# Decoder layer, quantised feed-forward stage: a maximum taken from the SBUF copy, a row of the final norm placed later, four banks for the last tiles

## The reference, cut to what matters

```python
def act_quant(x):
    scale = 127.0 / jnp.clip(jnp.max(jnp.abs(x), axis=-1, keepdims=True), EPS)
    return jnp.clip(jnp.round(x * scale), -128.0, 127.0) / scale

def h_bitlinear(x, w):                    # fwht: Hadamard transform of the last axis
    return jnp.einsum('bsh,oh->bso', act_quant(fwht(x)), weight_quant(w))

gate = h_bitlinear(hidden_states, w_gate)         # 512 -> 2048
up = h_bitlinear(hidden_states, w_up)
out = h_bitlinear(jax.nn.silu(gate) * up, w_down) # 2048 -> 512
...
x = _layernorm(x + _L0_attn_ref(...), axis=-1)
x = _layernorm(x + _L0_xattn_ref(...), axis=-1)
x = _layernorm(x + _L0_ffn_ref(...), axis=-1)
```

## Time and profile before

| | |
|---|---|
| median of 3 runs | 1088.88 us (1086.02 to 1090.52) |
| the profiled execution | 1086.8 us, of which 1084.9 from the first to the last instruction (the span) |
| TensorE busy | 936.8 us (86%) |
| VectorE busy | 875.3 us (81%) |
| ScalarE busy | 678.9 us (62.6%) |
| GpSimd busy | 231.3 us (21%) |
| mean granted TensorE clock | 0.959 of full speed |

### The profile page before, as it was taken

One profiled execution on the slowest core, in us unless ns is written; L12 is line 12 of the kernel. 1 busy time (PEld: TensorE's weight loads), 2 busy tenths in 40 slices (PEclk: granted clock), 3 DMA queues, 4 the chain that ended last, 5 costly groups with the idle time before them and its releaser, 6 DMA issues. The chain is left out here.

```text
span 1084.9 us, 13454 instructions
## 1 busy us (share of the span) xinstructions
PE 936.8 (86%) x4128; PEld 358.6 (33%) x4128; DVE 875.3 (81%) x1670; ACT 678.9 (63%) x1115; POOL 231.3 (21%) x248
## 2 busy tenths in 40 slices
PE   3567699999999999999898879897989889889966
PEld 1223233322222222222222444353444334343422
DVE  7997688899999999999897589658755776578467
ACT  3787688888888889877666234354524553275351
POOL 4203411122222331232201422140005000320001
PEclk9688899999999999999999999999999999999988
DMA  8956765566666556664442323120233004100501
GB/s 328 383 179 238 222 177 162 178 190 197 190 196 192 162 175 196 197 184 144 132 123 91 116 70 75 41 104 1 60 96 117 1 7 139 48 2 3 172 20 39
DMA packets 90684, 145.00 MB, mean 134 GB/s; under 512 B 12339, under 2 KB 52147, under 8 KB 89078
## 3 DMA queue, kind: packets, MB, share of 16 engines
q1 hardware_dynamic: 90614, 144.16, 42.3%
HBM read 84.75 MB, written 42.21 MB: 117 GB/s over the span
## 5 line engine op out<-in xcount | busy, mean ns | idle before, releaser
L402 DVE TENSOR_REDUCE neg_max<-banks 128x1 f32<-128x512 f32 x512 | 327.7, 682 | 32.8 <-PE banks L374 29.2
L1396 ACT ACTIVATE probs<-banks 128x512 f32<-128x512 f32 x512 | 277.1, 606 | 76.7 <-PE banks L1299 75.8
L1313 PE MATMUL banks<-probs,v_st 128*32 128x512 f32 x1024 | 137.9, 612 | 0.6 <-ACT probs L1396 0.6
L1850 PE MATMUL banks<-q_T,f_int_all 128*128 128x512 bf16 x512 | 122.9, 379 | 14.1 <-DVE h_ring L1871 10.1
L374 PE MATMUL banks<-attn_T,x_T 96*128 96x512 bf16 x256 | 98.6, 393 | 19.6 <-DVE neg_max L402 13.6
L1195 POOL TENSOR_TENSOR rstd<-vare,half 128x1 f32<-128x1 f32 x48 | 29.2, 608 | 401.1 <-DVE vare L1187 401.1
L1865 ACT ACTIVATE h_ring<-h_ring 128x512 f32<-128x512 f32 x64 | 40.3, 630 | 106.1 <-DVE h_ring L1860 106.1
L374 PE MATMUL banks<-k_st,q_st 96*128 96x512 bf16 x256 | 98.3, 384 | 7.8 <-DVE neg_max L402 6.4
L1299 PE MATMUL banks<-q_st,k_st 99*128 99x512 bf16 x256 | 96.0, 383 | 3.8 <-ACT probs L1396 1.8
L1299 PE MATMUL banks<-x_T,attn_T 99*128 99x512 bf16 x256 | 97.9, 382 | 0.1
L409 POOL TENSOR_TENSOR rest<-y,parts 128x512 f32<-128x512 f32 x32 | 37.6, 1174 | 211.7 <-ACT parts L382 211.6
(11 more groups left out here) (286 smaller groups left out, 1555.1 us busy)
## 6 DMA issues: line engine op xcount, KB each, us to landing
f_int_all<-in_ffn_dram SPq DMA_DIRECT2D x24, 512.0 KB, 7.6
qk_parts<-parts SPq DMA_DIRECT2D x32, 384.0 KB, 2.6
woT<-in_ffn_dram SPq DMA_DIRECT2D x24, 512.0 KB, 6.5
qk_parts<-parts SPq DMA_DIRECT2D x32, 256.0 KB, 2.9
pv_rows<-pv_z SPq DMA_DIRECT2D x32, 256.0 KB, 5.5
hz<-h_turned SPq DMA_DIRECT2D x32, 256.0 KB
x_T<-qk_parts SPq DMA_DIRECT2D x16, 384.0 KB, 3.9
attn_T<-qk_parts SPq DMA_DIRECT2D x16, 384.0 KB, 4.9
```

What stands on the lines that cost most here:

```text
L402: dve.tensor_reduce(neg_max[:, g.h, tile:tile + 1], s_bank[(16 * g.n + tile) % SB], AX.X, ALU.max, negate=True).then_inc(max_done, 1)
L1313: last = pe.matmul(pv_bank[32 * j:32 * j + 32, :], v_st[g.v][:, kt].rearrange("p h d -> p (h d)")[:, (HD + 1) * head:(HD + 1) * head + 2 * ...
L1396: act.activation(probs[ktp][:, j, i, :], st_bank[(16 * g.n + 2 * w + i) % STB], ACT.Exp).then_inc(exp_done, 2)
L1850: last = pe.matmul(bank, f_int[w][:, k * FF + ch.start:k * FF + ch.stop], q1_T[:, k, :], start=k == 0, stop=k == KD - 1)
```

## The change

Three things. **The maximum**: ScalarE no longer writes magnitudes; it only copies each pair into `hz`. VectorE reads the copy: one TENSOR_REDUCE takes the larger magnitude of the pair's two blocks, 1024 elements in, 512 out, through a view in which the two elements of each result lie 512 elements apart, and for every pair but the first a TENSOR_TENSOR of 128x512 puts it into `h_max`. The waits that named the magnitudes name the copy. **The row**: for b = 1 and 2 the final row 3 of batch b - 1 moves from step 15 of the first stage, where it stood ahead of the x2 read of row 0, to behind row 0's norm in the second stage; its scaling moves behind the x2 read of row 1, and its step on GpSimd moves with it. The x2 read now waits for the final row that used its own part of the buffer. **The last tiles**: in the last batch the four down tiles get four banks, and ScalarE rounds tiles 2 and 3, VectorE tiles 0 and 1.

```diff
@@ dve_xm
-            if n == 0:
-
-                need(dve, "d_read", 4 * (B - 1))
+            if B >= 2:
+                need(dve, "d_read", 4 * (B - 2) + n + 1)
@@ constants and banks
-            ACT_TILE, DVE_TILES = 2, (0, 1, 3)
+            ACT_TILES, DVE_TILES = (2, 3), (0, 1)
...
             def down_bank(b, t):
-                return psum[6 + t % 2] if b >= NB - 2 else LOW
+                return psum[t] if b == NB - 1 else psum[6 + t % 2] if b == NB - 2 else LOW
@@ pe_gate_up
                         if i < 2:
-                            need(pe, "h_abs", 8 * b)
+                            need(pe, "h2_sb", 8 * b)
@@ act_y
-                if i == KD:
-                    need(act, "maxed", 16 * b)
@@ pe_h2
                 else:
-                    need(pe, "h_abs", 8 * b + p - 1)
+                    need(pe, "h2_sb", 8 * b + p - 1)
@@ act_h2, dve_max
-            def magnitudes(p):
-                return h_abs[:] if p % 2 == 0 else y_own[:, 0:2, :]
-
             def act_h2(act, b, p):
                 need(act, "h2_mm", 8 * b + p + 1)
                 did(act.copy(hz[:, 2 * p:2 * p + 2, :], pair_banks(p)), "h2_sb")
-                need(act, "maxed", 16 * b + 2 * p - 2)
-                need(act, "bias_o_ready", 2)
-                did(act.activation(magnitudes(p), pair_banks(p), ACT.Abs), "h_abs")
 
             def dve_max(dve, b, p):
-                need(dve, "h_abs", 8 * b + p + 1)
-                for a in range(2):
-                    n = 16 * b + 2 * p + a
-                    need(dve, "maxed", n)
-                    if p == 0 and a == 0:
-                        need(dve, "top_mm", b)
-                        did(dve.tensor_copy(h_max[:], magnitudes(p)[:, a, :]), "maxed")
-                    else:
-                        did(dve.tensor_tensor(h_max[:], magnitudes(p)[:, a, :], h_max[:], ALU.max), "maxed")
+                need(dve, "h2_sb", 8 * b + p + 1)
+                if p == 0:
+                    need(dve, "top_mm", b)
+                out = h_abs[:, p % 2, :] if p else h_max[:]
+                did(dve.tensor_reduce(out, hz[:, 2 * p:2 * p + 2, :].rearrange("p a s -> p s a"), AX.X, ALU.max,
+                                      apply_absolute_value=True), "h_part")
+                if p:
+                    need(dve, "h_part", 8 * b + p + 1)
+                    need(dve, "maxed", 7 * b + p - 1)
+                    did(dve.tensor_tensor(h_max[:], out, h_max[:], ALU.max), "maxed")
@@ pe_top
-                need(pe, "maxed", 16 * b + 16)
-                need(pe, "h_abs", 8 * b + 7)
+                need(pe, "maxed", 7 * b + 7)
+                need(pe, "h2_sb", 8 * b + 7)
@@ act_half_q2
-                need(act, "q2_round", 2 * (NB - 1) + part + 1)
+                need(act, "q2_round", 2 * (NB - 1) + 2 * ACT_TILES.index(t) + part + 1)
@@ pe_down
-                    if b >= NB - 2:
+                    if b == NB - 1:
+                        need(pe, "h2_sb", 8 * NB)
+                    elif b == NB - 2:
@@ dve_first
-                    if b and down_end(b, i - 1) is not None:
+                    if b and i < FK - 1 and down_end(b, i - 1) is not None:
                         dve_final(dve, b - 1, down_end(b, i - 1))
...
                 dve_h(dve, b, FK - 1)
-                if b and b < NB - 1:
-                    dve_final_norm(dve, b - 1, KD - 1)
@@ dve_second
                 dve_xm_norm(dve, B, 0)
+                if b:
+                    dve_final(dve, b - 1, KD - 1)
                 dve_xm(dve, B, 1, FRONT)
+                if b:
+                    dve_final_norm(dve, b - 1, KD - 1)
@@ pool_second
                 pool_rstd(pool, 1, 4 * B)
+                if b:
+                    pool_final(pool, b - 1, KD - 1)
@@ the scalar block, last batch
-                    for part in range(2):
-                        act_half_round(act, ACT_TILE, part)
-                        act_half_q2(act, ACT_TILE, part)
+                    for t in ACT_TILES:
+                        for part in range(2):
+                            act_half_round(act, t, part)
+                            act_half_q2(act, t, part)
@@ the vector block, last batch
-                            if t != ACT_TILE:
+                            if t in DVE_TILES:
                                 dve_half_q2(dve, t, part)
```

More of the change, by code:

```diff
@@ L2003, in half_made @@
                 at = 2 * (NB - 1) + part + 1
-                return ("q2_ready", at) if t == ACT_TILE else ("q2_dve", at + 2 * DVE_TILES.index(t))
+                return ("q2_ready", at + 2 * ACT_TILES.index(t)) if t in ACT_TILES else ("q2_dve", at + 2 * DVE_TILES.index(t))
             def dve_half_scale(dve, t, part):
```

## The result

The changed kernel takes 1071.92 us (median of 4 runs, 1068.55 to 1077.68) against 1089.38 of the kernel before (4 runs, 1086.02 to 1090.52): a ratio of 0.986, 95% interval 0.983 to 0.988. The forecast was 1099 us, 0.9% slower. The profiled execution has a span of 1066.6 us against 1084.9.

A forecast was written before the change was run, and what follows sets the result against it. No engine is full; the chain goes to and fro between TensorE, ScalarE and VectorE. The terms 14.7 + 5.4 - 6.6 - 3.4 = 10.1 us slower gave 1099 us, range 1073 to 1111.

The forecast's parts named there:

- R: Duration of VectorE's new reduce, 1024 elements in, 512 out: taken as 1.98 us; break-even at 1.67.
- rival (a): VectorE's new reduce reads apart at the full rate, R = 1.21: 14.6 us won, 1074.3 us; chance 0.25.
- The three rows with inputs apart: Traced reduces with inputs 32 or 8 elements apart: 224 elements 0.529 us, 128 elements 0.369, 32 elements 0.207.
- The other sign: GpSimd's work next to VectorE's reduces lengthens them, by up to 0.4 us for each of three pairs.
- The second stages: Three second stages at R = 1.98: dve_quant2 starts at 34.25 us, not 29.34; 4.9 us lost each, 14.7 in all.
- the prediction's own walk: VectorE's second-stage list timed in order, gaps of 0.04 us; at R = 1.21, dve_quant2 comes 1.3 us earlier.
- Its slope: Between the ends, each second stage moves by eight times the change of R.
- A pair's pitch: VectorE's time per pair in a second stage: 1.98 + 0.69 + gaps, 2.74 us.
- The last pairs: Last batch's reduces and maxima on VectorE end at 1056.3, not 1050.93: 5.4 us lost, or 0.7 earlier at R = 1.21.
- The row: x2 read 1.80 us earlier; TensorE waits 1.2, not 3.02, eight matmuls 3.60, not 5.11: 6.6 us won in two stages.
- The last tiles: Last batch's tail: TensorE no longer waits for the final row; tile 3 ends at 1075.6, not 1079.0: 3.4 us won.
- rival (b): R from 1.5 to 1.84, two alternating places served better: within 5.4 us, taken as 1089; chance 0.12.

The follow-up runs named there:

- e4_probe: Changed kernel with twenty magnitude reduces added at its very end (one run); 224 elements in groups of seven took 0.54 us apart, 0.40 adjacent.
- e6_longer: Changed kernel with one more VectorE reduce per pair, 512 elements to 1, result not used: 1083.0 us, ratio 0.995 to the kernel before.
- e2: Kernel before with only final row 3 moved behind the x2 read: 1078.8 us, ratio 0.991.
- e1: Kernel before with only the maximum changed (ScalarE copies, VectorE reduces the copy): 1074.1 us against 1088.0, ratio 0.987.
- e11: Kernel before with only the maximum changed, plus unused matmuls put into TensorE's waits: 1069.3 us, ratio 0.981.
- e8: Changed kernel with unused matmuls put into TensorE's waits: 1062.9 us, ratio 0.977 to the kernel before.
- e7_probe2: Changed kernel with nineteen more VectorE instructions at its very end (one run); reduces in groups of 3 took 1.34 us, of 5 1.89.

## Why the prediction was wrong, step by step

**R.** The step that failed is "I take 1.98 us, from L215: a group of four is nearest to two". It is 1.23 us, and 1.21, the value of rival (a), was the one to take. The three rows with inputs apart were read rightly as slower for being apart (the line through them, 1.87 us for 1024, is what groups of four, eight and sixteen take in e4_probe to 0.03), but the rule was carried over to a group length that it doesn't hold for. The three rows differ from the new reduce in group length, and the prediction took the nearest length as near enough; groups of two, apart by 128 bytes, 2 KB or 16 KB, take what adjacent ones take. The other sign that the prediction named, reduces made longer by GpSimd's work beside them, did not come: all 32 took 1.22 to 1.24 us.

**The second stages.** Forecast 14.7 us lost; measured 0.6, 1.15 and 0.8, 2.6 us won. With R = 1.21 the prediction's own walk gave 1.3 each, 3.9. Without the lower clock a stage won 1.8, so the walk was too low there, and what the measured stages lack of it is the clock: the walk had TensorE slow only at the transposes, while in the changed kernel the slow stretch lay on the gate and up group ahead of them and held them up. Its slope, eight times the change of R, was too steep: e6_longer shows half against the changed kernel, and 0.7 of it against stages at full clock. Two terms of the walk were mis-sized. A pair's pitch at R = 1.23 is 1.87 and not about 2.0, since the gap ahead of an instruction without a wait is -0.08 and not 0.04 (the same holds in e6, 2.46 where the walk had 2.74). And VectorE had room in the middle of the list that the longer pairs fill first: in the changed kernel it still idles 8.3 us over 28 reduces for the copy, in e6 5.2. Even with R at 1.98 the whole would have come out near the kernel before and not 10 us above it: e6 took 1083.0 us, its pair is 0.16 us short of one with R = 1.98 (1.98 + 0.03 + 0.69 - 0.08 = 2.62), and the rest, scaled by what e6 showed (0.16 of 0.6, of 11 us), is an estimated 3 us more, against 1088.0 of the kernel before.

**The last pairs.** Forecast 5.4 lost at 1.98, 0.7 won at 1.21; measured 1.3 won, for the pitch of 1.87: from the end of the last norm to the end of the last maximum are 15.87 us before (1035.06 to 1050.93) and 14.57 after (1021.94 to 1036.51).

**The row.** Forecast 6.6, measured 6.4 in e2. Right in size and mechanism: 1.21 us of wait was forecast as 1.2, the matmuls as 3.60 and came at 3.67. But its second half was a price of the clock that only holds where the clock falls: with the waits filled the row is worth 1.8 a stage. On top of e1, whose profile has no slow stretch in q0 to T1 and q1 to T2, it gave 1.8 us in the first and 0.1 in the second, where the changed kernel's first down tile was slow.

**The last tiles.** Forecast 3.4, measured 3.42. Right, with the same reserve: where TensorE's waits in the tail are filled too, the edit is worth 1.6 us (30.56 in e11 to 28.92 in e8).

**What no step had.** Of the 18.3 us of span, 2.65 lie ahead of F, in code that is the same in both. By the clock 1.67 lie at the first down tile of batch 1 and 0.45 at the transposes of the last maximum (0.66 against 1.11 us, after a wait of 4.03 us and not 3.48). The sum by the table: 2.65 + 0.03 + 2.57 in second stages + 4.92 + 3.19 in q0 to T1 and q1 to T2 + 1.52 in q2 to q3 + 3.42 = 18.3. Rival (a) gave 14.6 and 1074.3 us, 2.4 above the measured median. Its R came, and 0.25 was too low a chance for it. Its reason, that the reduce reads apart at the full rate, holds for groups of two alone; the reason given for rival (b), that two alternating places are served better than four or seven, is nearer to what the probes show. That (a)'s sum lies so near is luck in part: it had 1.3 too much in the second stages, 0.6 too little in the last pairs, 1.5 too little in q0 to T1 and q1 to T2, where the one tile's clock went its way, and nothing for the 2.65 us ahead of F.

The counts above (nine of nine first down tiles slow with the old maximum, eleven of eighteen with the new one) and e1's gain of 14 us by the medians of six runs suggest that with the new maximum the clock falls less often behind the second stage, and more often inside it. They are only twenty-seven tiles in nine profiles, and why the clock moves so stays open: the profiles show where it fell, not why.

## What to carry to other kernels

Rows of the same kind of instruction price a new one only if they agree in the property that makes them dear; where they differ in two (distance and group length), the probe is twenty instructions at the end of a kernel and the range must hold both until then. Parts of a change that each shorten waits of TensorE do not add up, since each may save the same drop of the clock; price them with the waits filled, and look whether the filling reached every stage, which here it didn't. And a step that feeds another engine (quant1 for w1, with a copy queued behind it) goes ahead of work that nobody waits for: here that order and the filled waits were worth 16 us, as much as the whole change.

## What the runs showed of the hardware

- A magnitude reduce of 1024 elements in groups of two takes 1.23 us whether its inputs are adjacent, 128 bytes, 2 KB or 16 KB apart; in groups of three, 2 KB apart, 1.34; of four and more 1.87 to 1.90 when apart and 1.23 when adjacent.
- A run of 512 elements slows with its spacing in all three kinds tried. tensor_scalar took 0.44 us at a spacing of 1 and 2 elements and 0.63 at 4 and 8 (0.60 at 16); tensor_tensor, both inputs spaced, 0.70 and 0.70, then 1.07 and 1.07; the reduce to one result 0.70 and 0.70, then 1.06 and 1.08 (1.01 at 16). (All from e7_probe2.)
- The same eight f32 matmuls after the same wait of 3.02 us took 3.67, 5.11 or 6.72 us, by the granted clock. Filling TensorE's waits with unused matmuls gave 13.8 us in the kernel before and 9 in the changed one by the medians, 10.1 and 8.2 by the spans behind F.
- Two VectorE instructions, start to start: the duration of the first less 0.08 us where the second doesn't wait for the first, and plus 0.03 where it waits by a semaphore (shown for e6_longer).
